# The columns' t2 as a unit-matrix matmul on TensorE, with n, u and the input part of n in other PSUM banks

## The reference

```
r = sigmoid(xr + hr);  z = sigmoid(xz + hz)
n = tanh(xn + r * hn)
h = (1 - z) * n + z * h
```

## Time and profile before

| | |
|---|---|
| median of 3 runs | 2478.38 us (2475.55 to 2480.44) |
| profiled execution | 2490.38 us |
| its span | 2488.6 us |
| busy share of the span | PE 88%, DVE 81%, ACT 63%, POOL 62% |
| TensorE's mean granted clock | 0.985 |

### The profile page before, as it was taken

How to read it: one execution, slowest core, us unless ns; L and a number is a source line. 1 busy time by engine, 2 the same in 40 slices (tenths; PEclk the granted TensorE clock), 3 DMA queues, 4 the chain that set the end, 5 groups by cost and what they waited for, 6 DMA issues and landing times.

```text
span 2488.6 us, 79958 instructions
## 1 busy us (share of the span) xinstructions
PE 2186.1 (88%) x31528; PEld 1416.7 (57%) x31528; DVE 2014.4 (81%) x4982; ACT 1579.7 (63%) x3401; POOL 1532.9 (62%) x2114
## 2 busy tenths in 40 slices
PE   0579999899979999898979999899989999999995
PEld 0345555566646666565646666565656666555574
DVE  7309999877769999887869999887867888888874
ACT  0126666677758788676758888676757888666600
POOL 2007777667767677666767777666766777777600
PEclk9999999999999999999999999999999999999998
DMA  9993332256789997589999998589986665334699
GB/s 347 275 239 102 97 98 76 75 148 207 240 230 249 238 256 202 150 226 258 313 272 245 250 254 211 144 224 263 316 261 172 154 151 128 74 95 95 166 326 359
DMA packets 325716, 509.19 MB, mean 205 GB/s; under 512 B 24928, under 2 KB 140000, under 8 KB 325344
## 3 DMA queue, kind: packets, MB, share of 16 engines
q1 hardware_dynamic: 307296, 478.23, 70.1%
q10 hardware_dynamic: 18048, 25.85, 3.0%
HBM read 352.98 MB, written 151.01 MB: 203 GB/s over the span
## 4 chain that ended last, share of the span: by engine, by line
DVE 34%; PE 30%; ACT 17%; issue 8%; DMA 6%; POOL 3%; SPq 1%; ACTq 0%; DVEq 0%; POOLq 0%
PE bank L855 18%; DVE r L989 12%; DVE r L994 11%; ACT r L655 7%; DMA work<-x 5%; DVE h L1008 5%; ACT z L659 4%; ACT bank L663 3%; DVE bank L999 3%; PE bank L835 3%; PE bank L953 2%; ACT work L650 2%; PE bank L837 2%; DVE bn L981 1%; PE bank L856 1%
## 5 line engine op out<-in xcount | busy, mean ns | idle before, releaser
L855 PE MATMUL bank<-h,wh 64*64 64x256 f32 x6144 | 1498.8, 386 | 112.6 <-DVE h L1008 97.2
L835 PE MATMUL bank<-seq,wx 64*64 64x256 f32 x6144 | 1549.3, 385 | 43.6 <-DMA seq<-seq_next 21.6
L837 PE MATMUL bank<-seq,wx 64*64 64x256 f32 x6144 | 1549.9, 385 | 0.7 <-issue 0.7
L856 PE MATMUL bank<-h,wh 64*64 64x256 f32 x6144 | 1500.5, 387 | 0.2 <-issue 0.2
L537 POOL TENSOR_TENSOR v<-z,h 128x256 f32<-128x256 f32 x1024 | 747.0, 730 | 719.4 <-ACT z L659 693.2
L855 PEld LDWEIGHTS bank<-h,wh 64*64 64x64 f32 x6144 | 712.7, 133 | 577.4 <-DVE h L1008 409.2
L835 PEld LDWEIGHTS bank<-seq,wx 64*64 64x64 f32 x6144 | 755.2, 133 | 223.5 <-DVE r L994 119.1
L545 POOL TENSOR_TENSOR hsum<-hsum,h 128x256 f32<-128x256 f32 x1024 | 751.7, 734 | 117.7 <-DVE h L1008 98.4
L837 PEld LDWEIGHTS bank<-seq,wx 64*64 64x64 f32 x6144 | 752.7, 133 | 33.1 <-issue 4.2
L989 DVE SCALAR_TENSOR_TENSOR r<-bank,bhh,r 128x256 f32<-128x256 f32 x1024 | 490.0, 479 | 277.2 <-ACT r L655 236.5
L856 PEld LDWEIGHTS bank<-h,wh 64*64 64x64 f32 x6144 | 702.6, 133 | 0.8
(11 more groups left out here) (95 smaller groups left out, 2443.6 us busy)
## 6 DMA issues: line engine op xcount, KB each, us to landing
work<-x SPq DMA_DIRECT2D x384, 384.0 KB, 6.4
out<-work SPq DMA_DIRECT2D x192, 384.0 KB, 4.7
work<-x SPq DMA_DIRECT2D x143, 512.0 KB, 7.1
work<-x SPq DMA_DIRECT2D x286, 128.0 KB, 7.4
work<-x SPq DMA_DIRECT2D x32, 768.0 KB, 6.8
seq_next<-work SPq DMA_DIRECT2D x48, 512.0 KB, 6.7
work<-hsum_last SPq DMA_DIRECT2D x48, 512.0 KB, 7.5
seq<-x SPq DMA_DIRECT2D x17, 512.0 KB, 7.2
```

What stands on the lines that cost most here:

```text
L835: pe.matmul(as_pair(ps[LOW, :], c), wx[HIGH, gate, :], px[HIGH], start=start, stop=False, skip_group_check=True)
L837: return pe.matmul(as_pair(ps[HIGH, :], c), wx[LOW, gate, :], px[LOW], start=start, stop=False, skip_group_check=True)
L855: pe.matmul(ps[LOW, 0:N2], wh[LOW, gate, :], state[LOW], start=start, stop=True, skip_group_check=True)
L856: return pe.matmul(ps[HIGH, 0:N2], wh[HIGH, gate, :], state[HIGH], start=start, stop=True, skip_group_check=True)
```

## The change

The columns' t2 is no longer made on DVE. TensorE adds t1 to xn in PSUM instead: add_t1 multiplies t1 by the unit matrix ident, on the quarters LOW to LOW and HIGH to HIGH, after it has waited for t1. It stands in TensorE's order behind x_n of the next step's rows and the first unit_half or project_straight, and ahead of x_z of the next step's rows. gate_n of the columns reads PSUM.

For that, the columns' xn moves into the bank of hn (x_n starts the sum there and waits until n was made; h_n goes on with it), and n and u move into the second half of the bank of z. x_z of the columns therefore waits for the state, and stands behind h_r of the columns instead of ahead of it. x_r of the columns waits for r instead of t2. The rows keep their t2 on DVE.

```diff
--- before.py
+++ after.py
@@ -203,6 +203,9 @@
         rx_ps = [bank[0], bank[3]]
         hn_ps = [bank[1], bank[4]]
         z_ps = [bank[2], bank[5]]
+        xn_ps = [rx_ps[0][:, N2:2 * N2], hn_ps[1][:, N2:2 * N2]]
+        n_ps = [hn_ps[0][:, 0:N2], z_ps[1][:, N2:2 * N2]]
+        u_ps = [hn_ps[0][:, N2:2 * N2], z_ps[1][:, N2:2 * N2]]
         fin_ps = [bank[0:3], bank[3:6]]
         proj_ps = bank[6:8]
         next_ps = bank[6]
@@ -660,7 +663,8 @@
 
             def gate_n(g, t, c):
                 act.wait_ge(t2_ready[c], T * g + t + 1)
-                act.activation(hn_ps[c][:, 0:N2], r[:, c, :], ACT.Tanh, bias=bih[:, 2:3]).then_inc(n_ready[c], 1)
+                before = r[:, 0, :] if c == 0 else xn_ps[1]
+                act.activation(n_ps[c], before, ACT.Tanh, bias=bih[:, 2:3]).then_inc(n_ready[c], 1)
 
             def scan(g):
                 for t in range(T):
@@ -840,15 +844,19 @@
             def x_z(g, t, c):
                 if T * g + t > 0:
                     pe.wait_ge(z_ready[c], T * g + t)
+                if c == 1 and t > 0:
+                    pe.wait_ge(h_ready[1], state_before(g, t))
                 x_part(z_ps[c][:, 0:N2], 1, c, t, True).then_inc(x_z_ready[c], 1)
 
             def x_r(g, t, c):
                 if T * g + t > 0:
-                    pe.wait_ge(t2_ready[c], T * g + t)
+                    pe.wait_ge(t2_ready[0] if c == 0 else r_ready[1], T * g + t)
                 x_part(rx_ps[c][:, 0:N2], 0, c, t, True)
 
             def x_n(g, t, c):
-                x_part(rx_ps[c][:, N2:2 * N2], 2, c, t, False).then_inc(x_rn_ready[c], 1)
+                if c == 1 and T * g + t > 0:
+                    pe.wait_ge(n_ready[1], T * g + t)
+                x_part(xn_ps[c], 2, c, t, c == 1).then_inc(x_rn_ready[c], 1)
 
             def h_part(ps, gate, t, c, start):
                 state = h[:, c, (t + 1) % 2, :]
@@ -863,7 +871,14 @@
                 h_part(rx_ps[c], 0, t, c, False).then_inc(pre_r[c], 1)
 
             def h_n(g, t, c):
-                h_part(hn_ps[c], 2, t, c, True).then_inc(pre_n[c], 1)
+                h_part(hn_ps[c], 2, t, c, c == 0).then_inc(pre_n[c], 1)
+
+            def add_t1(g, t):
+
+                pe.wait_ge(t1_ready[1], T * g + t + 1)
+                pe.matmul(xn_ps[1][LOW], ident[LOW, :], r[LOW, 1, :], start=False, stop=True, skip_group_check=True)
+                pe.matmul(xn_ps[1][HIGH], ident[HIGH, :], r[HIGH, 1, :], start=False, stop=True,
+                          skip_group_check=True).then_inc(t2_ready[1], 1)
 
             def h_z(g, t, c):
                 pe.wait_ge(x_z_ready[c], T * g + t + 1)
@@ -896,9 +911,9 @@
                     h_n(g, t, 0)
                     x_n(g, t, 1)
                     h_z(g, t, 0)
+
+                    h_r(g, t, 1)
                     x_z(g, t, 1)
-
-                    h_r(g, t, 1)
                     if m is not None:
                         project_high(g + 1, m, 0)
                     if ends is not None:
@@ -921,6 +936,7 @@
                         project_straight(g + 1, m, 0)
                     if beside_input:
                         unit_half(g, u, 0)
+                    add_t1(g, t)
                     if t + 1 < T:
                         x_z(g, t + 1, 0)
                     if m is not None:
@@ -989,14 +1005,14 @@
                 dve.scalar_tensor_tensor(out=r[:, c, :], in0=hn_ps[c][:, 0:N2], scalar=bhh[:, 2:3], in1=r[:, c, :],
                                          op0=ALU.add, op1=ALU.mult).then_inc(t1_ready[c], 1)
 
-            def make_t2(g, t, c):
-                dve.wait_ge(t1_ready[c], T * g + t + 1)
-                dve.tensor_tensor(r[:, c, :], rx_ps[c][:, N2:2 * N2], r[:, c, :], ALU.add).then_inc(t2_ready[c], 1)
+            def make_t2(g, t):
+                dve.wait_ge(t1_ready[0], T * g + t + 1)
+                dve.tensor_tensor(r[:, 0, :], xn_ps[0], r[:, 0, :], ALU.add).then_inc(t2_ready[0], 1)
 
             def make_u(g, t, c):
 
                 dve.wait_ge(n_ready[c], T * g + t + 1)
-                dve.scalar_tensor_tensor(out=hn_ps[c][:, N2:2 * N2], in0=z[:, c, :], scalar=1.0, in1=hn_ps[c][:, 0:N2],
+                dve.scalar_tensor_tensor(out=u_ps[c], in0=z[:, c, :], scalar=1.0, in1=n_ps[c],
                                          op0=ALU.subtract, op1=ALU.mult).then_inc(u_ready[c], 1)
 
             def make_h(g, t, c):
@@ -1005,7 +1021,7 @@
                 dve.wait_ge(v_ready[c], k + 1)
                 if k >= 2:
                     dve.wait_ge(h_added[c], k - 1)
-                dve.tensor_tensor(h[:, c, t % 2, :], v[:, c, :], hn_ps[c][:, N2:2 * N2], ALU.subtract)\
+                dve.tensor_tensor(h[:, c, t % 2, :], v[:, c, :], u_ps[c], ALU.subtract)\
                    .then_inc(h_ready[c], 1)
 
             def add_x(g, u, k):
@@ -1030,7 +1046,7 @@
                 for t in range(T):
                     stats = g + 1 < PAIRS and t < CHUNKS
                     make_t1(g, t, 0)
-                    make_t2(g, t, 0)
+                    make_t2(g, t)
 
                     if stats:
                         half_chunk_stats(g + 1, t, 0)
@@ -1038,7 +1054,6 @@
                         add_x(g, unit_at[t - 1], 1)
                     make_t1(g, t, 1)
                     make_u(g, t, 0)
-                    make_t2(g, t, 1)
                     make_h(g, t, 0)
                     if stats:
                         half_chunk_stats(g + 1, t, 1)
```

## The result

The changed kernel takes 2561.8 us (2556.8 to 2565.7, four runs) against 2479.4 us of the kernel before beside it (2475.6 to 2480.6): a ratio of 1.033, 95% interval 1.030 to 1.035. Slower, as forecast, and 24 us above the forecast of 2538, within its range.

The account below looks back on a forecast made before the run. No engine was taken as full; a closed chain of waits sets the pace. Plain, unit, projection and remaining steps sum as -7 + 47 + 21 + 0 = +61, so 2478 + 60 = 2538 us, range 2484 to 2575.

Parts of the forecast that it names:

- Plain steps: First pass, 64 steps without extra work: nine-term columns' loop through TensorE, 3.95 us against 4.05; -7 us (0 to -12).
- Unit steps: 189 steps with x halves: moved x_z delays unit_half, so add_t1 is 0.40 late; 4.30 against 4.05, +47 us (+30 to +60).
- the forecast's chain: Unit step, columns' loop: state, h_r load, three crossed-pair matmuls, unit_half, add_t1, n, u, state; 4.30 us.
- Projection steps: Late parts of the passes that project, groups of seven steps: 30.25 against 29.2 us a group; +21 us (+8 to +35).
- High and straight: Steps with project_high and project_straight: straight waits for high_ready and stands before add_t1; 4.30 us a step.
- crossed alone: Steps with project_crossed only: the straight pair of array quarters stays free; 3.95 us a step.
- all three: Step with project_high, project_straight and project_crossed: 0.78 more than before's 4.72 us, so 5.50.
- Rest of the fourth pass: Its last 62 steps, with output units but no x halves: between -6 and +6 us, taken as 0.
- VectorE's busy time: Sign that the forecast is right: VectorE's busy time falls by 215 us, half of the 430.7 of all t2.
- Part 1: VectorE's u to state: 0.67 us with t2 between, 0.44 without; rows' loop would fall by 0.23, from 4.05 to 3.82.
- the faster one: Rival: the wait stays covered, add_t1 under 0.10 late, the shorter VectorE path decides; 2430 us, chance 0.13.
- The one by program order: Rival: matmuls start in program order over the quarters, add_t1 at 2.36 instead of 2.21; 2580 us, chance 0.07.

Follow-up runs that it names:

- The square: Kernel before, x_z of the columns moved alone (2505.4 us), add_t1 alone with columns' n and u in a spare PSUM bank to step 61 (2522.4 us), both (2561.8 us).
- the first x half in the gap: Changed kernel with first unit_x_half and first half of project_high moved ahead of h_r of the columns, while TensorE waits for the columns' state: 2510.1 us.
- one kernel: Changed kernel with columns' n and u in r's SBUF tile and x_z of the columns ahead of h_r again: 2671.8 us, ratio 1.078.

## Why the prediction was right, step by step

- *Plain steps*: right in kind, 3.87 where 3.95 was forecast, so -11 us in place of -7. The chain is the one that was named. In a plain step of the changed kernel the columns' state starts at 301.37, the weight load at 301.84, h_r's last pass at 302.11, r at 302.54, t1 at 303.05, add_t1 at 303.59, its last pass at 303.86 and n at 304.29; u and state follow after 0.48 and 0.47. None of the nine terms was off by more than 0.03, and most that were off were too large.
- *Unit steps*: confirmed in its place and size: 4.34 against 4.30, unit_half 0.45 behind the last crossed matmul against 0.44, add_t1 0.50 behind that against 0.48. 54 us against 47. The square shows the cause: x_z moved 4.09, add_t1 4.12, both 4.34. That the straight pair closes a chain of the same length was not seen, and that the two agree is chance: the forecast's chain alone would have had the unit steps of pass 3 shorten with add_t1 ahead of unit_half, and they grew by 0.20.
- *Projection steps*: the mis-sized term, 42 us against 21. High and straight (4.31 against 4.30), crossed alone (4.02 against 3.95) and all three (5.40 against 5.50) came near what was worked out. Missing were the steps that carry a unit as well. 16 crowded ones went from 4.46 to 5.19, 0.73 more, where high and straight was to grow by 0.27 (4.03 to 4.30): 7 us. 46 of crossed and unit went from 4.12 to 4.19, where crossed alone was to lose 0.08 (4.03 to 3.95): 7 us. The rest lies in the base: 7 x 4.17 was a window's mean with long steps in it; the seven steps themselves took 28.9, which is 0.3 less in each of 24 groups.
- *Rest of the fourth pass*: 0 forecast, -0.6 measured, and that is luck. The forecast took all 62 steps to carry a unit; 33 do, and they took 4.22 on average in place of 4.12, while those without one took 3.87 in place of 4.03.
- *VectorE's busy time*: down by 102 us where 215 was named as a sign. The rows of 512 t2 do add up to 215, but a t2 overlapped its neighbours and kept the engine for only 0.23 more of a step (0.67 against 0.44 in Part 1), which is 118 us in 512 steps, near the 102. The times forecast for a step do not rest on the 215.
- *Rivals*: the faster one falls: add_t1 is 0.29 later than t1 alone would let it be, 0.54 after t1's start as in the plain step (0.40 was forecast). The one by program order gave 2580 and is not what happened: h_z of the columns has its last pass at 894.17, x_r ahead of it in the program only at 894.54, and the unit steps follow the forecast's chain without that rule. That the measured time lies between the two forecasts has other reasons, the projection steps above all.

## What to carry to other kernels

Before work goes from one engine to another, list the closed chains of both and the passes of each array pair in every kind of step: here the gain (0.18 a step) was real in the steps without extra work, and was lost wherever either pair had some, so the move pays only in the plain steps. A change of two parts, each nearly harmless in a step, can cost when one delays what the other has put on the path; a square of four kernels shows it, and the undo must not bring a price of its own.

## What the runs showed of the hardware

Matmuls on different quarters start out of program order, but other engines see their ends as if they came in order. In the unit step above the columns' z starts at 894.99, 0.81 after h_z's last pass (894.17) and 0.45 after the last pass of x_r (894.54), which stands ahead of h_z in the program on the other pair; ACT had been idle for 0.61. In plain steps, where nothing ahead is late, it is 0.45; with x_r behind h_z 0.61 (unit_x_half is still ahead), with the first x half in the gap 0.45. In the plain and the unit steps of every kernel here with x_r ahead of h_z, z starts 0.44 to 0.47 after x_r's last pass (medians). The same holds for t1 behind h_n of the columns in pass 3: 0.67 in the changed kernel, where the first unit_x_half ahead of it ends later, 0.50 with that half in the gap or x_z back in its place. The Trainium skill (TensorE: Matmul & The Clock Gate, Part 3: Packing small matmuls) has starts and ends in program order: these runs agree for the ends as other engines see them, not for the starts. Neither z nor this t1 sets the pace of the changed kernel: with z's start 0.20 earlier it took 2559.0 us, nearly the same, and add_t1 waits longer than for t1.

VectorE was slower with all operands in SBUF than with one in PSUM: 585 against 421 ns for h in one kernel, 733 against 419 for u. GpSimd's add to the sum took 778 ns in that kernel and 734 in the one before. The runs don't say why.
